# One normalising pass for both heads of a pair: one exponential and one middle step on 128 partitions

## What is computed

```python
q_p = exp(q @ features.T - 0.5 * |q|^2) / sqrt(256)      # 12 heads of 64, 256 random features
kv, k_sum = k_p.T @ v, sum of k_p over the nodes         # computed in an earlier stage
out = q_p @ kv
normalizer = q_p @ k_sum
out = out / (normalizer + 1e-06)                         # the division that the change regroups
x_attn = out @ W_proj + b_proj
```

## Time and profile before

| | us |
|---|---|
| median of three runs | 2416.7 |
| the profiled execution's own time | 2420.72 |
| its span | 2419.0 |
| TensorE busy in the span | 2325.1 (96%) |
| VectorE busy | 1254.3 (52%) |
| ScalarE busy | 861.1 (36%) |
| on the chain that ended last: L1355, L1357, L1361 | 2%, 2%, 2% |
| the same: ScalarE's L956, L966 | 2%, 1% |

### The profile page before, as it was taken

How to read it: one execution, slowest core, us unless ns; L and a number is a source line. 1 busy time by engine, 2 the same in 40 slices (tenths; PEclk the granted TensorE clock), 3 DMA queues, 4 the chain that set the end, 5 groups by cost and what they waited for, 6 DMA issues and landing times.

```text
span 2419.0 us, 44796 instructions
## 1 busy us (share of the span) xinstructions
PE 2325.1 (96%) x16783; PEld 1585.8 (66%) x16783; DVE 1254.3 (52%) x2843; ACT 861.1 (36%) x1323; POOL 866.5 (36%) x615
## 2 busy tenths in 40 slices
PE   5999999999999999999999999999999999999597
PEld 3878787878666666676666666666665666666365
DVE  6757575745767676765214334434431544444444
ACT  3546464635747464552112222222220101111143
POOL 1001216567678787876631111111100000000266
PEclk9999999999999999999999999999999999999799
DMA  7888786653331313225237866777745655554287
GB/s 286 283 280 293 259 277 164 172 138 74 66 66 1 66 0 65 29 26 123 33 55 246 239 214 203 229 219 202 220 168 199 181 186 205 182 183 168 66 172 136
DMA packets 172421, 385.63 MB, mean 159 GB/s; under 512 B 74800, under 2 KB 81818, under 8 KB 166396
## 3 DMA queue, kind: packets, MB, share of 16 engines
q1 hardware_dynamic: 90220, 313.83, 37.7%
q0 software_dynamic: 71264, 40.45, 15.2%
q10 hardware_dynamic: 10800, 29.50, 3.3%
HBM read 222.76 MB, written 166.44 MB: 161 GB/s over the span
## 4 chain that ended last, share of the span: by engine, by line
PE 80%; DVE 7%; ACT 6%; issue 4%; DMA 2%; SPq 1%; POOL 0%; DVEq 0%; ACTq 0%; POOLq 0%
PE pair L1905 33%; PE pair L393 32%; PE pair L1721 5%; PE pair L1701 3%; PE pair L1651 2%; DVE arena L1355 2%; DVE arena L1361 2%; DVE arena L1357 2%; ACT arena L956 2%; PE pair L1710 1%; ACT arena L882 1%; DMA arena<-hl_dram,arena 1%; PE pair L1825 1%; PE pair L2042 1%; ACT arena L966 1%
## 5 line engine op out<-in xcount | busy, mean ns | idle before, releaser
L393 PE MATMUL pair<-arena 128*128 128x384 f16 (+3 forms) x5760 | 892.1, 316 | 5.3 <-issue 3.4
L747 POOL DMA_INDIRECT cells<-arena x392 | 656.1, 1674 | 559.1 <-DMA cells<-arena 413.1
L1905 PE MATMUL pair<-arena 128*128 128x384 f16 x4900 | 813.0, 326 | 0.9 <-DVE arena L1522 0.9
L393 PEld LDWEIGHTS pair<-arena 128*128 128x128 f16 x5760 | 563.7, 98 | 316.5 <-issue 6.6
L1905 PEld LDWEIGHTS pair<-arena 128*128 128x128 f16 x4900 | 473.6, 98 | 306.1 <-issue 1.2
L779 POOL DMA_INDIRECT slots<-arena x25 | 28.7, 1150 | 477.2 <-DVEq L1577 444.6
L1721 PE MATMUL pair<-arena 128*128 128x66 f32 x1200 | 155.7, 273 | 1.6 <-ACT arena L925 1.2
L925 ACT ACTIVATE arena<-pair,arena 128x256 f32<-128x256 f32 x300 | 125.8, 478 | 68.2 <-PE pair L1701 66.4
L1721 PEld LDWEIGHTS pair<-arena 128*128 128x128 f32 x1200 | 146.8, 193 | 4.3 <-ACT arena L925 1.5
L1029 ACT ACTIVATE arena<-arena 128x768 f32<-128x768 f32 x25 | 23.4, 935 | 333.8 <-DVE arena L1456 333.8
L765 POOL DMA_DIRECT2D arena<-cells x25 | 30.3, 1213 | 285.3 <-DMA arena<-cells 278.7
(11 more groups left out here) (202 smaller groups left out, 2447.7 us busy)
## 6 DMA issues: line engine op xcount, KB each, us to landing
cells<-arena SPq DMA_DIRECT2D x50, 800.0 KB
ahl_dram<-arena SPq DMA_DIRECT2D x23, 1600.0 KB, 11.0
arena<-ahl_dram SPq DMA_DIRECT2D x23, 1600.0 KB, 7.5
arena<-in_x SPq DMA_DIRECT2D x70, 384.0 KB
arena<-key_dram SPq DMA_DIRECT2D x28, 896.0 KB
arena<-cells SPq DMA_DIRECT2D x25, 800.0 KB, 7.6
arena<-cells POOLq DMA_DIRECT2D x25, 800.0 KB
split_w<-arena SPq DMA_DIRECT2D x32, 384.0 KB
```

What stands on the lines that cost most here:

```text
L393: ins = nc.tensor.matmul(dst[half], left(k, a), right(k, b, half), start=start and n == 0, stop=stop and n == 2)
L747: nc.gpsimd.indirect_dma_start(cells[k], bass.IndirectOffsetOnAxis(ap=idx_all[:, m:m + 1], axis=0), val_all[:, m:m + 1], None, bounds_chec ...
L1905: ins = nc.tensor.matmul(pair[u][:, half, 0:HD], a[:, 0, s * P:(s + 1) * P], X[part][:, s, half * HD:(half + 1) * HD], start=(s == 0 and p ...
```

## The change

ScalarE's `normaliser(c, p, h)` becomes `log_sums(c, p, h)`, once for each head, and `normaliser(c, p)`, once for the pair: the two logarithms are written to the two halves of `ln_den`, and one exponential on 128 partitions follows. Both `square_high` of the next pair stand ahead of them. VectorE's `normalise(c, p)` handles both heads: D for head 0, D for head 1, one M on 128 partitions, A for head 0, A for head 1; both `square_low` stand ahead. `den` is one buffer in place of two, and the semaphore counts follow (3 in place of 4 for a pair). TensorE's list is the same.

```diff
--- before.py
+++ after.py
@@ -210,7 +210,7 @@
         ss = [at(RX + 1200 + CW * (2 + u), 2, CW, dt=F16) for u in range(2)]
         sq = at(RX + 7600, CW)
         qp_sb = at(RX + 4400, 4, CW)
-        den = [at(RX + 3760, CW), at(RX + 17502 + CW, CW)]
+        den = at(RX + 3760, CW)
         ln_den, q_rows = at(RX + 17502, CW), at(RX + 6960, CW)
         a_f = at(RX + 8240, CW)
         aT = [at(RX + 8880 + 1920 * part, PAIRS, CW, dt=F16) for part in range(2)]
@@ -956,18 +956,19 @@
                 nc.scalar.activation(halves_of(qp_sb[:, g, :], c),
                                      bank_pair(1 + s, c), ACT.Exp).then_inc(qp_free[s], 1)
 
-            def normaliser(c, p, h):
+            def log_sums(c, p, h):
                 m = c * PAIRS + p
                 s, j = q_use[("o", p, h)]
                 act.wait_ge(qp_full[s], c * q_uses[s] + j + 1)
-                rows = ln_den[(1 - h) * DH:(2 - h) * DH]
                 if h == 0 and (not isinstance(m, int) or m):
                     act.wait_ge(a_ready, 2 * m)
-                nc.scalar.activation(halves_of(rows, c), bank_pair(1 + s, c)[DH:P],
+                nc.scalar.activation(halves_of(ln_den[h * DH:(h + 1) * DH], c), bank_pair(1 + s, c)[DH:P],
                                      ACT.Ln, bias=eps6[DH:P, 0:1]).then_inc(den_ready, 1)
-                act.wait_ge(den_ready, 4 * m + 2 * h + 1)
-                n = 2 * half_cols(c)
-                nc.scalar.activation(den[h][DH:P, 0:n], rows[:, 0:n], ACT.Exp, scale=-1.0).then_inc(den_ready, 1)
+
+            def normaliser(c, p):
+                m, n = c * PAIRS + p, 2 * half_cols(c)
+                act.wait_ge(den_ready, 3 * m + 2)
+                nc.scalar.activation(den[:, 0:n], ln_den[:, 0:n], ACT.Exp, scale=-1.0).then_inc(den_ready, 1)
 
             def attn_high(c, p):
                 m = c * PAIRS + p
@@ -991,10 +992,10 @@
                         q_high(*nxt, 1)
                         q_square(*nxt)
                         square_high(*nxt, 0)
-                    normaliser(c, p, 0)
-                    if next_up:
                         square_high(*nxt, 1)
-                    normaliser(c, p, 1)
+                    log_sums(c, p, 0)
+                    log_sums(c, p, 1)
+                    normaliser(c, p)
                 attn_high(c, PAIRS - 1)
 
             nc.scalar.preload_act_table_set("natural_log_exp_and_others")
@@ -1346,29 +1347,31 @@
             dve.wait_ge(sq_done, 1)
             newton(cs, dinv, deg[:, 0:T], t25[:, 0, :], t25[:, 2, :])
 
-            def normalise(c, p, h):
-                m = c * PAIRS + p
-                s, j = q_use[("o", p, h)]
-                cn = Chain(dve, dve_done, c * (q_links + y_links) + (q_base + 4 * p + 2 * h))
-                dve.wait_ge(den_ready, 4 * m + 2 * h + 2)
-                n = 2 * half_cols(c)
-                cn.link(nc.vector.scalar_tensor_tensor(halves_of(ln_den[DH:P], c), bank_pair(1 + s, c)[DH:P], 1e-6,
-                                                       halves_of(den[h][DH:P], c), ALU.add, ALU.mult))
-                cn.link(nc.vector.scalar_tensor_tensor(den[h][0:DH, 0:n], ln_den[DH:P, 0:n], 2.0, den[h][DH:P, 0:n],
+            def normalise(c, p):
+                m, n = c * PAIRS + p, 2 * half_cols(c)
+                cn = Chain(dve, dve_done, c * (q_links + y_links) + (q_base + 3 * p))
+                dve.wait_ge(den_ready, 3 * m + 3)
+                for h in range(2):
+                    s, rows = q_use[("o", p, h)][0], slice(h * DH, (h + 1) * DH)
+                    cn.link(nc.vector.scalar_tensor_tensor(halves_of(ln_den[rows], c), bank_pair(1 + s, c)[DH:P], 1e-6,
+                                                           halves_of(den[rows], c), ALU.add, ALU.mult))
+                cn.link(nc.vector.scalar_tensor_tensor(den[:, 0:n], ln_den[:, 0:n], 2.0, den[:, 0:n],
                                                        ALU.subtract, ALU.mult))
-                if h == 0 and (not isinstance(m, int) or m):
+                if not isinstance(m, int) or m:
                     dve.wait_ge(a_lo, m)
-                nc.vector.scalar_tensor_tensor(halves_of(a_f[h * DH:(h + 1) * DH], c), bank_pair(1 + s, c)[0:DH], -1.0,
-                                               halves_of(den[h][0:DH], c), ALU.mult, ALU.mult).then_inc(a_ready, 1)
-                dve.wait_ge(a_ready, 2 * m + h + 1)
-                dve.sem_inc(qp_free[s], 1)
+                for h in range(2):
+                    s, rows = q_use[("o", p, h)][0], slice(h * DH, (h + 1) * DH)
+                    nc.vector.scalar_tensor_tensor(halves_of(a_f[rows], c), bank_pair(1 + s, c)[0:DH], -1.0,
+                                                   halves_of(den[rows], c), ALU.mult, ALU.mult).then_inc(a_ready, 1)
+                    dve.wait_ge(a_ready, 2 * m + h + 1)
+                    dve.sem_inc(qp_free[s], 1)
 
             def attn_low(c, p):
                 dve.wait_ge(a_hi, c * PAIRS + p + 1)
                 n = 2 * half_cols(c)
                 nc.vector.tensor_tensor(aT[1][:, p, 0:n], a_f[:, 0:n], aT[0][:, p, 0:n], ALU.subtract).then_inc(a_lo, 1)
 
-            q_links, y_links = 4 * PAIRS, 3 * TC
+            q_links, y_links = 3 * PAIRS, 3 * TC
             q_base = links(q_links + y_links, C)
 
             def chunk3(c, first=False, more=True):
@@ -1381,12 +1384,10 @@
                             attn_low(c, p - 1)
                         q_low(*nxt)
                         square_low(*nxt, 0)
+                        square_low(*nxt, 1)
                     elif p:
                         attn_low(c, p - 1)
-                    normalise(c, p, 0)
-                    if next_up:
-                        square_low(*nxt, 1)
-                    normalise(c, p, 1)
+                    normalise(c, p)
                 attn_low(c, PAIRS - 1)
                 if first:
                     dve.wait_ge(rows_in, 16)
```

## The result

The changed kernel takes 2423.74 us (median of nine runs, 2420.55 to 2427.49) against 2416.92 for the kernel before in the same comparison: a ratio of 1.0023, 95% interval 1.0013 to 1.0033. It is slower by 6.8 us by the medians, 5.6 by the ratio. The forecast was 2414.5, range 2410.5 to 2421, so the measured time lies above the range.

What follows compares the result with a forecast made beforehand. The prediction took TensorE (12.47 us a pair) and, just above it, the ScalarE-VectorE loop (13.14, falling to 12.79) as limits. Gains of 8.0 us less losses of 5.8 gave -2.2 us, so 2414.5, range 2410.5 to 2421.

Steps and rivals of the forecast that it cites:

- The views and the bound: Stage of the change: TensorE's own work is 12.47 us a pair, the loop through ScalarE and VectorE takes 13.14.
- VectorE's side of the loop: From the end of the exponential to the end of the last A: 4.39 us in place of 6.14, 1.75 less.
- Ln 0 to Ln 1 ... 0.67: ScalarE, start to start of the two logarithms: 0.67 us, with an overlap of 0.12 taken from two feature exponentials.
- The upper end: The two logarithms without any overlap, 0.81 us apart: gains 5.0, losses 6.5, sum +1.5 us.
- Together 8.0 us: Gains: 5.6 us in full rounds of chunks 0 to 3, 1.2 in their first waits, 1.2 in chunk 4.
- The losses: Slot 1 given back later: 3.8 us at the ends of chunks 0 to 3, 2.0 in chunk 4, together 5.8.
- Rows 1: Row matmuls behind the last pair of chunks 0 to 3 wait for slot 1: 0.96 us each, 3.8 in all.
- F1 in the last pair: Chunk 4, pair 5: this feature product waits for slot 1 and starts 2.0 us later, after some 4.6 us idle.
- F1 in the other pairs: Slot 1 comes free 0.15 us late for this feature product; costs nothing, as the slack before F2 is 0.17.
- The clock: Rival: TensorE's clock falls after the idle in chunk 4's last pair, +1.7 to +3.4 us, 2416.2 to 2417.9; chance 0.32.
- the loop is not shorter: Rival: logarithms or 128-partition steps cost 0.35 us a pair more, gains vanish, +7.5 us, 2424; chance 0.08.
- low part hidden anyway: Rival: the low part moved ahead on VectorE was already hidden; half the gain, +1 to +3 us; chance 0.08.

Runs made afterwards that it cites:

- the first experiment: Kernel before the change, with both square_high and both square_low of the next pair moved ahead of the unchanged per-head normalisation: 2414.43 us, ratio 1.0002.
- the wait filled: Changed kernel plus 20 matmuls that nobody reads, ahead of F1 in the last pair of chunk 4: 2416.05 us, ratio 1.0010 to the kernel before.

## Why the prediction was wrong

**The views and the bound: right.** TensorE's own 12.47 us against a loop of 13.1 through ScalarE and VectorE. The cast moved to VectorE showed it: with the loop shortened, the round stopped at 12.46.

**VectorE's side of the loop: right.** 4.40 us against 4.39, with A to A at 0.97 (752.08 to 753.05). The rule of the Trainium skill that was weighed there (VectorE: DVE Perf Modes, section The DRAIN you can't avoid: a semaphore after each op costs nothing extra) does not cover a semaphore instruction of its own, as it stands here behind A: D to D, with one wait between, is 0.86 us; A to A, with a wait and an increment, 0.97; A to D in the first experiment, with a further wait, 1.03.

**"Ln 0 to Ln 1 ... 0.67": the first step that failed.** It measured 0.82. I took the spacing from two feature exponentials, which read and write from partition 0 both times. The logarithms write to different halves. This is 0.15 of the 0.19 us by which the loop was set too short (12.79 where it is 12.98); the rest is 0.01 to 0.02 each in the casts, the exponential and VectorE's steps. The upper end that I gave for this step, 0.81, was the true one.

**"Together 8.0 us": the term that failed, by more than that step.** The gains were 3.2 (2.8 in chunks 0 to 3, 0.4 in chunk 4). Besides the logarithms, I had compared with one round of 13.14 where the neighbours are at 13.11, the cast before Ln 0 takes 0.75 and not 0.73, and the first rounds of the chunks shortened by 0.13 and not by 0.3. Each is small, but there are 24 of them, and the whole gain was a small difference of large sums. The sum at my upper end still had gains of 5.0. Of the 8.6 us between forecast (-2.2) and stage (+6.4), the gains are 4.9, the losses 1.1 and the clock 2.6.

**The losses: right in kind and place.** Rows 1 at 0.96 each: the stretches grew by 1.15 to 1.19, as the loop's error of 0.19 us lets the slot come free that much later. F1 in the last pair, 2.0 us later: 2.25. F1 in the other pairs was late by some 0.28 us rather than 0.15, and cost nothing by itself, as said, because F2 still waited behind it. That five places hold the whole loss was then shown by putting the old order back in them.

**The clock: a term that the sum put at nothing.** The sum ran F1 and the tile at full speed behind an idle of 4.6 us; the fall was a rival, given 0.32 and 1.7 to 3.4 us. It happened and cost 2.63. The row of an idle of 3.7 us followed by the low level stood against one of 2.5 at full speed, and 4.6 lay above both, so I hold now that the forecast should have carried it. In the runs 2.54 us idle kept the clock in two traces, 2.64 lost it in one, and after 3.2 it fell only in the tile. The Trainium skill (TensorE: Matmul & The Clock Gate, Part 1) has the gate fall back after idling, at a point that depends on phase; these rows fit that, but no run here tests the phase.

With the gains at 3.2, the losses at 6.9 and the clock at 2.6 the sum is +6.4 (6.38 from the unrounded terms). The range ended at +4.3 over the median, since it set the clock on top of an upper end that was itself too low.

**The rival "the loop is not shorter"** gave 2424, and the nearness to 2423.74 is in good part luck. Its cause was half right: the logarithms in different halves did cost more. But the loop was shorter, by 0.14 us, F1's lateness did not reach F2, and without the fall of the clock, which this rival does not have (as with the wait filled), the kernel stood only 3.0 us over the one before.

**The rival "low part hidden anyway"** is wrong in its mechanism. The second low part stood in the loop: it ran from 755.91 to 756.73, and D of head 1 began at 756.76. Taking it out shortened VectorE's side by 0.77 us; what ate the gain is the cast that went ahead of the logarithm in its place.

## What to carry to other kernels

When several steps of a pipeline are merged, ask when each of its buffers is given back, and look at the places where the consumer has nothing else in front: here 24 rounds gained 0.13 us each and five places gave back three times as much. In a loop through two engines, look first for work that can leave it: here regrouping gave some 3 us at most, while one cast moved to the engine that idled at that moment gave 12 us. And where a change lengthens an idle of TensorE, its clock belongs in the price: here it came to 1.5 to 2.6 us behind a single idle of 2.64 to 4.8 us.

## What was not expected of the hardware

- Two ScalarE instructions in a row overlap by 0.10 to 0.12 us (two feature exponentials 1.28 us, two logarithms into the same half 1.48) or not at all (two logarithms into different halves 1.61, two casts of different halves 1.47 for a single one of 0.72). In these rows the overlap goes with the first partition of what is read and written being that of the instruction before. For the logarithms the experiment shows it, for the output (the tile changed with it); for the casts it is read from the rows and wasn't tried. One more row fits: in the earlier trace rows the cast of head 1, which reads and writes from partition 64, starts 0.64 us after an exponential of 0.73 that does the same (752.47, 753.11). The Trainium skill (ScalarE: Activation LUTs, section What ACT_TABLE_LOAD costs) has an overlap of 93 ns for ACTIVATEs back to back, without this condition; where instructions overlap here, the rows come close to the figure; where the halves differ, they show no overlap.
- A cast of 64 x 640 numbers from 32 to 16 bits took 0.49 us on VectorE and 0.72 on ScalarE.
- TensorE's clock fell after idles of 2.64, 3.2, 4.1 and 4.8 us ahead of F1 in the last pair, and not after 2.54 in two traces. Why 2.64 was enough in one execution stays open; a single trace of each kernel can't show how often it falls.
